# Attention over one core: a PSUM bank moved from the ring of the products for maxima to the ring of the scores

## The reference

```
q, k, v = proj(Wq), proj(Wk), proj(Wv)          # b = 2, 8 heads, 2304 tokens, 16 channels
scores  = einsum('bhqd,bhkd->bhqk', q, k) / 4
attn    = softmax(scores)
out     = einsum('bhqk,bhkd->bhqd', attn, v);  z = out @ Wo.T;  x = x + z
```

## Time and profile before

| | us |
|---|---|
| median of 3 runs | 2243.61 (2240.99 to 2244.31) |
| the profiled execution, whole | 2243.17 |
| its span, first to last instruction | 2241.3 |
| windows with their maxima, first to last reduction | 1113.6 to 2174.6 |
| PE busy, share of the span | 79% |
| DVE busy, share of the span | 78% |
| ACT busy, share of the span | 51% |

### The profile page before, as it was taken

How to read it: one execution, slowest core, us unless ns; L and a number is a source line. 1 busy time by engine, 2 the same in 40 slices (tenths; PEclk the granted TensorE clock), 3 DMA queues, 4 the chain that set the end, 5 groups by cost and what they waited for, 6 DMA issues and landing times.

```text
span 2241.3 us, 36271 instructions
## 1 busy us (share of the span) xinstructions
PE 1775.6 (79%) x12208; PEld 1003.2 (45%) x12208; DVE 1751.3 (78%) x4342; ACT 1136.6 (51%) x2902; POOL 1146.7 (51%) x1269
## 2 busy tenths in 40 slices
PE   4444444468888876444599999999999999999998
PEld 2444444435454543444435555555534444444433
DVE  5777777769999985777598888887888888888871
ACT  3333333320000003333448888888777777777776
POOL 3777777726666664777587777777231000000000
PEclk8667666669999998666779999999999999999999
DMA  7666666600000006666443433343001111111101
GB/s 248 206 206 206 205 206 206 205 16 1 1 1 1 1 5 201 205 206 208 102 126 100 115 107 105 105 114 107 14 9 28 28 23 24 26 23 20 22 1 43
DMA packets 90664, 211.60 MB, mean 94 GB/s; under 512 B 18544, under 2 KB 43760, under 8 KB 90352
## 3 DMA queue, kind: packets, MB, share of 16 engines
q0 software_dynamic: 51840, 169.91, 25.3%
q1 hardware_dynamic: 38640, 39.38, 8.0%
HBM read 174.62 MB, written 13.37 MB: 84 GB/s over the span
## 4 chain that ended last, share of the span: by engine, by line
PE 42%; ACT 4%; issue 2%; DVE 2%; POOL 1%; DMA 0%; SPq 0%; ACTq 0%; POOLq 0%
PE ps L1385 13%; PE ps L1349 13%; PE ps L1363 11%; ACT l_e L1095 3%; PE ps L1442 2%; PE ps L1432 1%; PE ps L1370 1%; DVE l_mx L1219 1%; ACT corner L1066 1%; PE ps L1396 1%; POOL l_part L963 0%; PE ps L1402 0%; POOL corner L953 0%; PE ps L1423 0%; PE ps L1409 0%
## 5 line engine op out<-in xcount | busy, mean ns | idle before, releaser
L1219 DVE TENSOR_REDUCE l_mx<-ps 128x1 f32<-128x384 f32 x1728 | 835.6, 549 | 129.7 <-PE ps L1363 129.6
L1095 ACT ACTIVATE l_e<-ps 128x384 f32<-128x384 f32 x1728 | 726.1, 511 | 217.4 <-PE ps L1349 215.5
L1363 PE MATMUL ps<-l_ka,l_qs 96*128 96x384 bf16 x1728 | 572.0, 334 | 13.9 <-DMA l_qs<-l_part 9.4
L1349 PE MATMUL ps<-l_qs,l_ks 99*128 99x384 bf16 x1728 | 565.3, 330 | 10.3 <-ACT l_e L1095 4.6
L253 POOL DMA_INDIRECT l_corner<-table,l_idx x324 | 315.4, 973 | 129.2 <-issue 98.1
L418 DVE SCALAR_TENSOR_TENSOR l_samp<-l_corner,l_wts,l_samp 128x128 f32<-128x128 f32 x972 | 284.9, 348 | 111.4 <-ACT l_samp L336 103.7
L1385 PE MATMUL ps<-l_e,l_v_s 128*32 128x384 f32 x3456 | 331.2, 491 | 1.6 <-ACT l_e L1095 0.8
L649 DVE SCALAR_TENSOR_TENSOR l_prod<-ps,c_b,l_pad 128x384 f32<-128x384 f32 x588 | 312.3, 609 | 25.0 <-PE ps L684 25.0
L1349 PEld LDWEIGHTS ps<-l_qs,l_ks 99*128 99x128 bf16 x1728 | 166.3, 97 | 365.0 <-ACT l_e L1095 192.9
L512 PE MATMUL ps<-l_turned,l_wk 128*128 128x128 f32 x648 | 146.2, 419 | 213.0 <-ACT l_turned L344 213.0
L585 POOL TENSOR_TENSOR l_prod<-l_prod 128x1152 f32<-128x1152 f32 x84 | 221.3, 2635 | 140.6 <-DVE l_prod L649 140.6
(11 more groups left out here) (169 smaller groups left out, 1894.9 us busy)
## 6 DMA issues: line engine op xcount, KB each, us to landing
table<-l_tok SPq DMA_DIRECT2D x16, 640.0 KB, 6.6
l_ka<-l_part SPq DMA_DIRECT2D x96, 72.0 KB
l_ks<-l_part SPq DMA_DIRECT2D x96, 72.0 KB
l_corner<-table,l_idx POOLq DMA_INDIRECT x324, 3.7
l_qs<-l_part SPq DMA_DIRECT2D x96, 48.0 KB, 2.1
corner<-table,idx POOLq DMA_INDIRECT x270, 3.6
l_qs<-l_part SPq DMA_DIRECT2D x96, 24.0 KB
out<-x_map SPq DMA_DIRECT2D x12, 192.0 KB, 1.9
```

Source lines behind the costliest of these rows:

```text
L1095: nc.scalar.activation(e[:, w % 2, i, :], ps[:, st_bank(at), 0:QC], ACT.Exp).then_inc(s["st_free"], 1)
L1219: nc.vector.tensor_reduce(mx[:, ga % MAX_SLOTS, u // NQC, u % NQC:u % NQC + 1], ps[:, ab_bank(at), 0:CH], AX.X, ALU.max) \
L1349: nc.tensor.matmul(ps[:, bank, 0:QC], ks[:, head % 2, kt * 128:(kt + 1) * 128], qs[:, gb % 3, j * QC:(j + 1) * QC], start=True, stop=True) \
L1363: nc.tensor.matmul(ps[:, bank, 0:CH], qs[0:KROWS, ga // CT % 3, q0:q0 + 128], ka[:, head % 2, k0:k0 + CH], start=True, stop=True).then_inc ...
```

## The change

Of the seven banks below bank 7 the scores' ring gets four (0 to 3) instead of three, and the ring of the maxima gets three (4 to 6) instead of four (3 to 6). No instruction is added or removed, and their order on every engine stays. Only the distance at which TensorE waits for a reader changes: one entry more for the scores' ring, one entry less for the other.

```
-ST_RING, AB, AB_RING, AV = 3, 3, 4, 7
+ST_RING, AB, AB_RING, AV = 4, 4, 3, 7
```

## The result

The changed kernel takes 2307.35 us in the median (2304.54 to 2308.15), against 2242.70 (2240.99 to 2244.31) for the kernel before in the same comparison: 1.0286 of it, 95% interval 1.0268 to 1.0304. The forecast was 2303. The profiled execution has a span of 2305.0 instead of 2241.3, 63.7 more, and the same 36271 instructions.

A forecast was written before the change was run, and what follows sets the result against it. The prediction took ScalarE's loop (4.31 us a plain window) as the bound, with VectorE's at 4.22 growing to 4.68. Terms 38.7 + 27 + 0 + 1 - 6.6 = +60 on 2243.2 gave 2303; 8-in-10 range 2274 to 2318.

The forecast's parts named there:

- Two loops 0.09 apart: Plain window before the change: ScalarE's cycle through exponentials 4.31 us, VectorE's through reductions 4.22, only 0.09 below.
- The 4.31: ScalarE's cycle in a plain window before, from the exponential of score 3 to that in the next window, in us.
- The 4.22: VectorE's cycle with four maxima banks, summed in us from reduction 4 through reduction 7 and the burst to reduction 4.
- The plain windows: Windows 108 to 204, no convolution beside: each from 4.31 to 4.68 us, +3.6 a batch, +38.7 in all.
- The release delay: From a reduction's end to the maximum product that takes its bank: 0.05 us, ScalarE's value taken for VectorE too.
- The convolution beside: Windows 0 to 85, work between score 5 and maximum product 6: 48.3 to 51.2 us a batch, +27 in all.
- The rival in which this stretch would cover the longer loop: Longer waits in windows 0 to 85 cover the fourth reduction pitch, so only plain windows lengthen: 2276 us, chance 8%.
- The windows 86 to 107: Mixed windows: gains of perhaps 0.5 us in six with projections, losses elsewhere; taken as 0, between -3 and +3.
- The last windows: From window 205, no maxima: fourth score bank brings bursts from 4.88 to 4.15 us, or 4.15 to 3.87; sum -6.6.
- The stretch of maxima alone: Before window 0, paced by VectorE: at most one reduction pitch at each of three turn_samples, 0 to +1.4, taken +1 us.
- The faster rival: Scores' ring was the bound: up to 0.21 us less in each of 205 windows and 6.6 at the end; 2194, chance 4%.
- the clock rival: TensorE falls to 1.2 GHz: +3.5 us a window, up to 700; if a tenth of the windows, 2373; chance 2%.

The follow-up runs named there:

- The halved reductions: Each reduction over 192 of 384 columns, queries scaled by a further 1/16: 2200.15 us with rings of four and three, 2234.07 with three and four.
- banks by stage: Kernel before, but rings of four and three in windows 90 to 95, five and two from window 206 on: 2232.48 us, 0.9954 of the kernel before.
- the burst earlier: Changed kernel with the burst one place earlier, maximum product 3 behind it: 2303.22 us, 1.0272 of the kernel before.
- the burst cut: Half of the burst's products moved ahead of score 7 of the same window: 2250.54 us with rings of four and three, 2258.15 with three and four.
- the late banks only: Kernel before, but rings of five and two from window 206 on: 2234.20 us, 0.9957 of the kernel before.

## Why the prediction was right, and where it was not

**What bounds.** Two loops 0.09 apart was the reading on which all rested. The 4.31 is a row. The 4.22 stays a sum, since with four banks for the maxima no plain window was below 4.31; it is borne out one pitch further, where the sum gives 4.68 and the row 4.71. The halved reductions show both from the other side: with VectorE's loop set free a window stays at ScalarE's 4.31 with three score banks, and falls to TensorE's 4.17 with four.

**The plain windows.** Forecast 4.68, measured 4.71; forecast 43.8 a batch, measured 43.9 to 44.0. The terms hold: from the start of r4 (1907.16) to the burst (1909.90) 2.74 against 1.86 + 0.55 + 0.05 + 0.26 = 2.72, 1.43 for the burst, 0.54 to r4. The release delay, taken from ScalarE, was good for VectorE.

**The convolution beside.** Forecast +27, measured +26.0. The rival in which this stretch would cover the longer loop gave 2276 and fell; the loop is shifted by that work and not hidden by it.

**The windows 86 to 107.** Forecast 0, measured +1.2, by two parts of opposite sign as reasoned: the seven intervals from the burst of window 90 went from 43.3 to 41.5, and the four ahead of them from 22.0 to 24.5. What I hadn't seen is in those four: in one of them the clock fell, at the end of this text. That the sum is near 0 is in part luck, since nothing had been worked out for the size of either part but the 0.5 in six windows, 3 in all, and the seven intervals gave 1.8.

**The last windows.** Forecast -6.6, measured -6.0: the intervals with a z tile went to 4.15 as said, but the first two in the batch, 4.30 and 4.47, didn't quite, against 4.90 and 5.21.

**The stretch of maxima alone, and window 0.** Forecast +1, at most +1.4; measured +3.7. This is the term that was mis-sized, since it left out the clock. From the first reduction to the start of the 90th it is 46.4 before and 48.7 after (46.3 and 46.4 with banks by stage, 48.7 with three and three, 47.6 with the burst earlier, 47.5 with rings of four and three and the burst cut). The copies of the turned samples show what the ring costs there:

```profile
1146.36 0.56 DVE L1247 COPY l_turned<-ps 128x384 f32<-128x384 f32 x1 [0.81 <-PE ps L1432]
...
1152.01 0.56 DVE L1247 COPY l_turned<-ps 128x384 f32<-128x384 f32 x1 [0.56 <-PE ps L1432]
...
1157.51 0.56 DVE L1247 COPY l_turned<-ps 128x384 f32<-128x384 f32 x1 [0.77 <-PE ps L1432]
```

They are 5.65 and 5.50 apart, and 5.04 both times before. I had bounded each of the three by one pitch, and the two intervals kept to that nearly, 0.6 and 0.5. The first copy comes 33.2 after the first reduction, and 32.1 before. These 1.1 aren't the ring's. At the start of the stretch reductions come 0.75 apart and not 0.47 while TensorE is at the 1.2 GHz level, and that lasts for seven of them after and for three before:

```profile
1116.00:1119.00 3.00, 3.00 (x24) 2.87 (x22) 2.90 (x7) 2.49 (x11) 1.72 (x1) 0.96 0.17 43
...
1116.00:1119.00 3.00, 3.00 (x15) 2.73 (x14) 2.23 (x4) 1.68 (x8) 1.51 (x1) 0.53 0.16 41
```

The first row is of the kernel before, the second of the changed one: 0.96 and 0.53. The number doesn't go with the ring: there are seven such steps with five banks for the maxima too, and three with three banks in the two kernels above that take 47.5 and 47.6. So of the 2.3 the ring costs 1.2, inside the forecast, and the clock, which rose later, costs 1.1.

The other part is the clock in window 0:

```profile
1160.00:1165.00 5.00, 4.33 (x16) 1.63 (x17) 4.96 (x13) 2.90 (x6) 4.61 (x4) 0.82 0.54 157
1165.00:1170.00 5.00, 5.00 (x30) 3.52 (x29) 2.50 (x6) 3.36 (x10) 4.78 (x7) 0.84 0.01 2
```

Before, both stretches are at 1.00. From the 90th reduction to the burst of window 1 it is 8.2 after and 6.8 before. In the kernel with the late banks only, whose rings are those of before here, it is 9.4, with the clock at 0.56 from 1160 to 1165. With three banks for the maxima it is 9.9, 8.6 and 9.1 (three and three, burst earlier, burst cut). So this part isn't the ring's alone, and how much of it is these runs don't say.

**The faster rival.** It fell, and what the Trainium skill says in "Perfetto Trace Analysis", section "Optimization Strategy", was no guide to which ring should have the bank. The repeated gap ahead of the scores did mean too few banks, as the page says that it can: with shorter reductions the fourth bank takes most of it away (28.8 us of waits for exponentials from 1740 to 2100, against 81.4 with three) and gains 34 us. But the page speaks of one gap, and here the bank had to come from a ring whose loop was only 0.09 shorter by the sums. The measurement decides: +65 us.

**The forecast of the sizes beyond one bank.** The loop with a fixed pitch failed in the experiments with a ring of two, as told above: it left out that the round trip through two banks can be longer than two pitches, 0.92 for two exponentials against 0.76.

## What to carry to other kernels

Price a ring of banks as a loop: from the release that the last product ahead of the longest unbroken work (here the burst) waits for, through that work, to the reader of the first product behind it, then the reader's pitches up to the one that releases the bank again, and its full duration. The pitches are the products of a window, less the banks, less one: 8 - 4 - 1 = 3 and 8 - 3 - 1 = 4 here. In a ring of two, look first whether the round trip through it is longer than two pitches. Do so for every ring that shares the banks, before the sums of waits are read: a ring that waits 81 us and one that waits 2 were 0.09 us a window apart by these sums. Where stages differ in what they want, the banks can follow the stage, but an exchange at a moment when a reader is behind gives back what it wins.

## What the runs showed of the hardware

Behind window 0 the granted clock fell in the changed kernel in one place, at the statistics of the second image. The windows view and TensorE's timeline there:

```profile
1655.00:1658.00 3.00, 1.77 (x9) 0.34 (x6) 2.90 (x9) 1.89 (x5) 0.00 (x0) 1.00 0.00 0
1658.00:1661.50 3.50, 3.50 (x22) 1.40 (x22) 1.35 (x3) 1.05 (x3) 0.00 (x0) 0.51 0.00 0
1661.50:1665.00 3.50, 3.06 (x17) 1.29 (x15) 2.94 (x10) 3.05 (x6) 0.78 (x4) 1.00 0.00 0
...
1657.09 0.34 PE L1363 MATMUL ps<-l_ka,l_qs 96*128 96x384 bf16 x1 [1.23 <-DVE l_mx L1219]
...
1658.66 2.77 PE L1385 MATMUL ps<-l_e,l_v_s 128*32 128x384 f32 x13
1661.36 0.39 PE L1349 MATMUL ps<-l_qs,l_ks 99*128 99x384 bf16 x1
```

TensorE had been idle for 1.23 waiting for a reduction, and was busy for 1.77 of the 3 us before; then the clock was granted at 0.51, the 1.2 GHz level, and the burst took some 2.9 instead of 1.43. The window took 6.97, against 5.03 before the change and 5.50 with rings of three and three, where the clock didn't fall. So behind window 0 the clock rival was real in one window, at a cost of 1 to 2 us, and it did not spread: the plain windows that followed stayed at 1.00 with a wait in each. The same happened at the exchange of rings above (0.72 and 0.62 in the windows view of 1643 to 1645 and 1645 to 1648). In the kernel before, no such fall begins in the windows 1 to 215, nor does one with three and three, the burst earlier, the halved reductions or the late banks alone. The kernels with rings of two and five, of five and two, and both with the burst cut have one or two each, so it isn't tied to three banks for the maxima: ahead of one with three and four and the burst cut, a score had waited 2.05 for an exponential, and with two and five 2.91.
